# Attention: the denominators' products directly behind a pair's value products, and the maxima negated by a two-input instruction

## What is computed

```python
scale = HEAD_DIM ** (-0.5)                      # 16 heads of 32
q, k, v = (to_tokens(q), to_tokens(k), to_tokens(v))          # 4096 tokens
attn = jax.nn.softmax(jnp.einsum('bhnd,bhmd->bhnm', q, k) * scale, axis=-1)
out = jnp.einsum('bhnm,bhmd->bhnd', attn, v)
out = out.transpose(0, 1, 3, 2).reshape(B, C, H, W)
out = conv1x1(out, wo, bo)
return (out + q_in) / jnp.sqrt(jnp.float32(2.0))
```

## Time and profile before

| | |
|---|---|
| time, median of 3 runs | 5617.67 us (5606.56 to 5618.09) |
| the profiled execution | 5617.22 us, of it the span of the trace 5615.4 us |
| TensorE busy | 5180.6 us (92%) |
| VectorE busy | 4026.3 us (72%) |
| ScalarE busy | 2729.0 us (49%) |
| GpSimd busy | 3104.6 us (55%) |
| TensorE's granted clock, mean | 0.967 of full speed |

### The profile page before, as it was taken

How to read it: one execution, slowest core, us unless ns; L and a number is a source line. 1 busy time by engine, 2 the same in 40 slices (tenths; PEclk the granted TensorE clock), 3 DMA queues, 4 the chain that set the end, 5 groups by cost and what they waited for, 6 DMA issues and landing times. The chain is left out here.

```text
span 5615.4 us, 98850 instructions
## 1 busy us (share of the span) xinstructions
PE 5180.6 (92%) x31784; PEld 2477.6 (44%) x31784; DVE 4026.3 (72%) x5231; ACT 2729.0 (49%) x5079; POOL 3104.6 (55%) x1336
## 2 busy tenths in 40 slices
PE   7989999999999999999999999999634899999977
PEld 3434444444444444444444444444212455555433
DVE  3238888888888888888888888888312677876633
ACT  1115666666666666666666666666400244344401
POOL 0006888888888888888888888888600000000000
PEclk9988999999999999999999999999867999999989
DMA  3230101011001010100010101000133000100164
GB/s 145 105 106 9 26 12 25 12 25 24 13 24 25 12 26 13 25 24 14 23 26 12 25 12 25 24 13 10 43 106 107 10 30 17 34 21 29 40 186 153
DMA packets 103213, 225.84 MB, mean 40 GB/s; under 512 B 14768, under 2 KB 23984, under 8 KB 99632
## 3 DMA queue, kind: packets, MB, share of 16 engines
q1 hardware_dynamic: 98464, 211.79, 12.5%
q10 hardware_dynamic: 4368, 8.65, 0.4%
HBM read 139.39 MB, written 80.48 MB: 39 GB/s over the span
## 5 line engine op out<-in xcount | busy, mean ns | idle before, releaser
L655 DVE TENSOR_REDUCE b_mx<-b_pmax 128x1 f32<-128x512 f32 x4096 | 2566.9, 682 | 535.1 <-PE b_pmax L511 532.4
L632 ACT ACTIVATE b_prob<-b_pscore 128x512 f32<-128x512 f32 x4096 | 2155.5, 602 | 1329.6 <-PE b_pscore L525 1324.5
L491 POOL TENSOR_TENSOR b_sums<-b_sums,b_prob 128x1024 f32<-128x1024 f32 x1024 | 2442.8, 2386 | 531.5 <-DVE b_sums L680 358.7
L511 PE MATMUL b_pmax<-b_kst,b_qst 96*128 96x512 f32 x4096 | 1773.2, 436 | 52.7 <-DVE b_mx L655 31.1
L525 PE MATMUL b_pscore<-b_qst,b_kst 98*128 98x512 f32 x4096 | 1658.4, 406 | 20.5 <-issue 12.8
L511 PEld LDWEIGHTS b_pmax<-b_kst,b_qst 96*128 96x128 f32 x4096 | 779.9, 190 | 1126.2 <-DVE b_mx L655 983.0
L538 PE MATMUL b_pout<-b_prob,b_vst 128*32 128x512 f32 x8192 | 1095.8, 607 | 0.0
L525 PEld LDWEIGHTS b_pscore<-b_qst,b_kst 98*128 98x128 f32 x4096 | 778.3, 190 | 396.3 <-issue 227.4
L485 POOL TENSOR_TENSOR b_sums<-b_prob 128x1024 f32<-128x1024 f32 x256 | 612.4, 2392 | 451.9 <-ACT b_prob L632 447.2
L1258 DVE SCALAR_TENSOR_TENSOR d_dsum<-d_ypad,d_dw,d_dsum 128x2048 f32<-128x2048 f32 x288 | 681.7, 2367 | 10.2
L1041 POOL TENSOR_TENSOR d_num_w<-d_vks,d_mask 128x128 f32<-128x128 f32 x8 | 5.6, 699 | 762.9 <-ACT d_vks L1219 762.9
(11 more groups left out here) (115 smaller groups left out, 2191.6 us busy)
## 6 DMA issues: line engine op xcount, KB each, us to landing
b_kst<-scratch_kh SPq DMA_DIRECT2D x32, 512.0 KB, 9.3
b_qst<-scratch_qh SPq DMA_DIRECT2D x128, 128.0 KB, 2.5
scratch_att<-b_outn SPq DMA_DIRECT2D x128, 128.0 KB, 2.3
scratch_num<-d_num SPq DMA_DIRECT2D x64, 256.0 KB, 2.0
f_num<-scratch_num SPq DMA_DIRECT2D x8, 2048.0 KB, 10.2
f_rden<-scratch_rden SPq DMA_DIRECT2D x64, 256.0 KB, 9.5
a_x<-in_x SPq DMA_DIRECT2D x4, 2048.0 KB, 14.7
scratch_qh<-a_high SPq DMA_DIRECT2D x8, 1024.0 KB, 4.0
```

Of the source, the lines that this page charges most:

```text
L491: pool.tensor_tensor(acc, acc, p[:, step, :], ALU.add).then_inc(pool_added, 1)
L511: pe.matmul(pmax[max_bank(place_of(u, m))][:], qst[0:SUMS, b, t * P:(t + 1) * P], kst[0:SUMS, par, j * BANK:(j + 1) * BANK], start=True, s ...
L632: act.activation(prob[:, kt % PBUF, half * BANK:(half + 1) * BANK], pscore[score_bank(hs)][:], ACT.Exp, scale=SCALE).then_inc(exped, 1)
L655: dve.tensor_reduce(mx[:, t, j:j + 1], pmax[max_bank(place_of(u, m))][:], AX.X, ALU.max).then_inc(max_read, 1)
```

## The change

Two edits, both in `stage_attention`.

In TensorE's program the block that issues the denominators is written ahead of the fourth maximum product and of the transposition instead of behind them. So at the end of an octave's last pair the four D products follow the four V products directly, and M3 follows D.

In VectorE's program the negation of the maxima (L664) becomes a `scalar_tensor_tensor` that computes (m x -2) + m, with `mtop` as both inputs, where a `tensor_scalar` with one input computed m x -1. Its result is the same number, rounded in the same way.

```diff
                             times_v(u - 1, head, par if c else 1 - par, (c - 1) % UNITS, PAIRS - 1)
-                        for m in products[3:]:
-                            max_product(u + ahead, m, t_par, t_buf)
-                        if pair == PAIRS - EARLY and not (final and place == TURN - 1):
-                            transpose_shift(u + 1)
                         if pair % (OCT // 2) == OCT // 2 - 1:
                             o = pair // (OCT // 2)
                             if o:
                                 denominators(u, o - 1)
                             elif behind:
                                 denominators(u - 1, OCTS - 1)
+                        for m in products[3:]:
+                            max_product(u + ahead, m, t_par, t_buf)
+                        if pair == PAIRS - EARLY and not (final and place == TURN - 1):
+                            transpose_shift(u + 1)
...
                 dve.wait_ge(max_mm, done(u * SLOTS + T_AT + 1))
-                dve.tensor_scalar(mneg[:, 0:QT].bitcast(F32R), mtop[:], -1.0, None, ALU.mult).then_inc(mlink, 1)
+                dve.scalar_tensor_tensor(mneg[:, 0:QT].bitcast(F32R), mtop[:], -2.0, mtop[:], ALU.mult,
+                                         ALU.add).then_inc(mlink, 1)
                 small(u, 2)
```

## The result

The changed kernel takes 5717.66 us, the median of 4 runs (5707.94 to 5728.9), against 5612.82 for the kernel before in the same comparison (4 runs): a ratio of 1.0188, 95% interval 1.0162 to 1.0214. It is slower, as forecast, but by 105 us and not by 62, and the time lies above the range, which ended at 5705. The profiled execution took 5710.98 with a span of 5709.2, 93.8 more than the span before.

The account below looks back on a forecast made before the run. TensorE, busy for 98% of attention, was taken as the bound. 62 units x (0.55 + 0.29) = 52, copies +13 - 3, negation 0 gave +62 us on 5617.2: 5679, range 5580 to 5705.

Parts of the forecast that it names:

- TensorE alone: Pair with D in attention: 3.92 us in place of 4.24, a gain of 0.32 for 250 groups, 80 us.
- The stall behind D: Pair after D: TensorE waits for VectorE, 0.50 us in three octaves, 0.33 in the one with an unheld addition.
- The ring: VectorE's addition and GpSimd's five wait for each other: held additions end 13.63 us apart, each growing to 1.38.
- Pair 14 and the copy: TensorE waits longer for VectorE: 0.29 us in each unit's pair 14, 0.84 at each of 15 copies of values.
- The negation: VectorE's L664 in its new form stays held by GpSimd's addition: gain 0.
- The sum: Whole kernel: 62 units x (0.55 + 0.29) = 52, copies +13 - 3, negation 0: +62 us, 5679.
- VectorE's waits for M were to shrink: Sign expected in the profile after: VectorE's waits for TensorE's maximum products shrink; no size given.
- more backlog: Rival: a late M3 also delays the pair after, 0.3 us in each of 186 held octaves: 5735 us, chance 0.06.
- The negation was not freed: Rival judged: GpSimd no longer holds L664, which falls to some 0.17 us: 5586 us, faster, chance 0.16.
- the gain was not had in full: Rival judged: VectorE catches up before the next M3, so the order saves all 80 us: 5537 us, chance 0.06.
- gain and stall did not cancel: Rival judged: GpSimd never behind, addition stays 1.21 us, octave +0.01, pair 14 unchanged: +15 us, 5632, chance 0.09.
- the point named for D: Start of the D that needs GpSimd's fifth addition, 2543.68 + 13.45; that addition was said to end some 4 us ahead.

Follow-up runs that it names:

- the early addition: Changed kernel with VectorE's addition put ahead of its fourth maximum read in the octave's last pair: 5541.15 us, 0.9876 of the kernel before.
- the old order with the early addition: Kernel before, its order kept, with VectorE's addition put ahead of its fourth maximum read: 5678.66 us, 1.0115 of the kernel before.

## Why the prediction was wrong in size and right in kind

- *TensorE alone.* 3.92 forecast, 3.93 measured; 80 us forecast, 73 shown once all else was out of the way. Right, a little high.
- *The stall behind D.* Forecast 0.50 in three octaves and 0.33 in the free one; the pairs behind D take 3.57, 3.49, 3.58 and 3.41 in the medians, so 0.50, 0.42, 0.51 and 0.34 over 3.07. Right. That it is VectorE's lost pause is shown by the early addition, which removes it.
- *The ring.* Forecast 13.63 us between held additions. The additions above end 13.61 apart (2549.52 and 2563.13), at 1.28 and 1.35 us, a little under the 1.38 forecast; by octaves the three held ones take 1.37, 1.30 and 1.39 in the medians. Right.
- *Pair 14 and the copy.* +0.29 and +0.84 forecast, +0.27 and +0.8 measured. Right.
- *The negation.* 0 forecast, 1.0004 measured. Right; the 2.32 us of L666 in the old order with the early addition shows this operation at this size held, which the trace before could show only for larger ones.
- *The sum.* It failed here. It took every microsecond of TensorE at the clock of the earlier trace rows, 1.00, and asked of each longer wait only how long it is. That a wait of 1.38 in place of 0.61 can be followed by a stretch at half clock, as it was in 9 of the 15 copy units, stood in no term and in no rival; such stretches, with those at pair 14, are some 23 of the 94 us of the profiled execution. The range, which ended 26 us above the forecast, had no room for it.
- *A sign that failed.* VectorE's waits for M were to shrink. They became fewer, but 115 us longer in all: VectorE now idles while V and D run, 1.45 above where it was 0.57. The first line is before, the second after (us in all, times, longest):

```profile
DVE b_mx L655 <- PE b_pmax L511: 532.4, 901, 4.5
DVE b_mx L655 <- PE b_pmax L511: 647.3, 697, 4.5
```

- *The rivals.* The nearest to the time, "more backlog" (5735), had a wrong mechanism: the pair after the stalled one takes 3.06. The negation was not freed, the gain was not had in full, and gain and stall did not cancel.
- *A reading.* GpSimd's fifth addition ends 5 us ahead of the point named for D, by the prediction's own numbers, and not "some 4"; nothing hangs on it.

Why the clock falls behind some waits and not behind others of the same length (the copy's, and those of 0.7 at pair 14) is not explained by these runs; nor is how many of them a run gets, though the changed kernel's runs spread over 21 us.

## What to carry to other kernels

A group of products that stands between two products of one chain is also the pause in which the chain's reader does its other work: before moving it, walk the reader through one period, and move its other work into the new pause with it. Where the work of two engines cannot overlap, as VectorE's and GpSimd's additions here, add up what they do in a period: here 13.6 us an octave, though before the change GpSimd was busy for 85% of attention and VectorE for 84%. And price a longer wait of TensorE twice, for its length and for the clock that may fall behind it.

## What the runs showed of the hardware

- A 128 x 8 instruction of VectorE with two inputs in SBUF took 0.17 us free and 2.32 behind a GpSimd addition that started 0.07 us ahead of it; one of 8 x 128 with one of its two inputs in PSUM took 0.28 beside such an addition.
- Products with zero weights in the copy's wait, of which some 0.5 us stayed idle in place of 1.38, kept TensorE at full clock in all 15 copy units: 58.0 us a unit in place of 59.4 to 59.7 where it had fallen.
